# A graph-and-FFN kernel: the self-loop is added before the window's matmuls, GpSimd's order of work is turned round, and each edge gather gets its index copied first

## The reference

```
edge_index = stack([src, dst])                  # 206250 edges, sorted by dst
# graph layer on layernorm(x):
src, dst = edge_index + self-loops of all nodes
norm = dinv[src] * dinv[dst]                    # dinv = rsqrt(degree)
h    = layernorm(x) @ W
out  = segment_sum(h[src] * norm, dst) + b
x    = x + where(out > 0, out, prelu_a * out)
# FFN on layernorm(x): softmax router over 8 experts, the top 2 for all nodes,
# gelu(z @ W1[e] + b1[e]) @ W2[e] + b2[e], weighted sum, layer norm
x    = x + ffn(layernorm(x))
```

## Time and profile before

| | |
|---|---|
| median of 3 runs | 1114.66 us (1113.95 to 1115.24) |
| the profiled execution, its own time | 1114.66 us |
| its span in the profile | 1112.8 us |
| TensorE busy | 1082.8 us, 97% |
| VectorE busy | 935.0 us, 84% |
| GpSimd busy | 672.9 us, 60% |
| ScalarE busy | 537.8 us, 48% |
| the 40 windows | from about 84 us to 791 us |

### The profile page before, as it was taken

One profiled execution on the slowest core, in us unless ns is written; L12 is line 12 of the kernel. 1 busy time (PEld: TensorE's weight loads), 2 busy tenths in 40 slices (PEclk: granted clock), 3 DMA queues, 4 the chain that ended last, 5 costly groups with the idle time before them and its releaser, 6 DMA issues.

```text
span 1112.8 us, 21292 instructions
## 1 busy us (share of the span) xinstructions
PE 1082.8 (97%) x6833; PEld 930.4 (84%) x6834; DVE 935.0 (84%) x2198; ACT 537.8 (48%) x1367; POOL 672.9 (60%) x584
## 2 busy tenths in 40 slices
PE   6999999999999999999999999999899999999997
PEld 5787887888888888888888888888699999999997
DVE  6898888989989899898998998986468787878785
ACT  5794443444434444443444444444375564656451
POOL 3103677888888888888888888882124342434332
PEclk9999999999999999999999999999999999999999
DMA  8076454555455555555545555552211111111101
GB/s 281 17 293 217 117 145 134 154 148 162 137 150 147 152 157 145 162 145 155 154 138 159 145 154 146 153 146 76 81 59 58 44 42 46 48 39 52 38 24 33
DMA packets 65527, 134.96 MB, mean 121 GB/s; under 512 B 10388, under 2 KB 35870, under 8 KB 65438
## 3 DMA queue, kind: packets, MB, share of 16 engines
q0 software_dynamic: 29040, 93.22, 30.0%
q1 hardware_dynamic: 36398, 40.62, 11.2%
HBM read 108.14 MB, written 25.67 MB: 120 GB/s over the span
## 4 chain that ended last, share of the span: by engine, by line
PE 83%; DVE 6%; ACT 4%; issue 3%; DMA 1%; POOL 1%; DVEq 1%; ACTq 0%; POOLq 0%; SPq 0%
PE bank L1776 40%; PE bank L1753 14%; PE bank L1907 11%; PE bank L1794 8%; PE bank L1894 5%; PE bank L1644 2%; DVE gl L1344 2%; PE bank L1879 1%; ACT zf L1562 1%; ACT gf L1577 1%; POOL rstdf L797 1%; DMA W<-in_W 1%; ACT gh L1575 1%; PE bank L1741 1%; PE bank L1634 1%
## 5 line engine op out<-in xcount | busy, mean ns | idle before, releaser
L703 POOL DMA_INDIRECT row<-h_table,lists x315 | 435.3, 1382 | 101.1 <-issue 71.0
L1776 PE MATMUL bank<-tab,adj 128*128 128x512 f32 x1960 | 476.0, 392 | 1.1 <-ACT adj L1510 1.1
L1505 ACT CAST adj<-bank 128x392 fp32r<-128x392 f32 x624 | 258.0, 501 | 398.6 <-PE bank L1753 398.6
L1776 PEld LDWEIGHTS bank<-tab,adj 128*128 128x128 f32 x1960 | 366.4, 188 | 82.1 <-DVE tab L1021 1.2
L1126 DVE TENSOR_TENSOR hot_key<-iota_key,turned 128x588 bf16<-128x588 bf16 (+1 forms) x480 | 243.6, 559 | 0.0
L1118 DVE TENSOR_TENSOR hot_src<-iota_src,turned 128x1536 bf16<-128x1536 bf16 x160 | 157.6, 985 | 53.5 <-PE bank L1753 52.1
L1753 PEld LDWEIGHTS bank<-hot_key,hot_src 128*128 128x128 bf16 x1872 | 157.5, 145 | 40.9 <-issue 29.3
L1753 PE MATMUL bank<-hot_key,hot_src 128*128 128x147 bf16 x1872 | 185.5, 248 | 0.0
L1344 DVE TENSOR_TENSOR gl<-gf,gh 128x384 fp32r<-128x384 f32 (+1 forms) x136 | 116.8, 886 | 29.5 <-ACT gf L1577 29.1
L1575 ACT ACTIVATE gh<-bank,b1e 128x384 fp32r<-128x384 f32 (+1 forms) x136 | 78.3, 575 | 97.6 <-PE bank L1894 97.5
L1907 PE MATMUL bank<-W2h,gh 128*128 128x256 f32 x392 | 112.2, 286 | 0.0
(11 more groups left out here) (230 smaller groups left out, 1334.0 us busy)
## 6 DMA issues: line engine op xcount, KB each, us to landing
h_table<-tab SPq DMA_DIRECT2D x5, 2048.0 KB, 8.8
x1f<-x_dram POOLq DMA_DIRECT2D x16, 384.0 KB, 3.8
out<-res SPq DMA_DIRECT2D x48, 128.0 KB
xin<-in_x SPq DMA_DIRECT2D x45, 128.0 KB, 3.4
x_dram<-x SPq DMA_DIRECT2D x45, 128.0 KB
row<-h_table,lists POOLq DMA_INDIRECT x315, 3.8
xs<-in_x SPq DMA_DIRECT2D x2, 1536.0 KB, 15.1
h_table<-tab SPq DMA_DIRECT2D x1, 2304.0 KB, 14.3
```

What stands on the lines that cost most here:

```text
L703: g.indirect_dma_start(out=row[:, u, :].bitcast(F32), out_offset=None, in_=h_table, in_offset=bass.IndirectOffsetOnAxis(ap=lists[:, m % 2, ...
L1505: s.copy(adj[k][:, :].rearrange("p (q n) -> p q n", n=P)[:, :, at:at + GN], adj_ps[j][:, 0:KEYS].rearrange("p (n q) -> p q n", q=T)).then_ ...
L1776: last = mm(acc[k][:, :], adj[k][:, q * P:(q + 1) * P], tab[:, q, :], start=(at == 0), stop=(at == T - 1), skip_group_check=True)
```

## The change

Three things are changed. `load_edges(i)` first copies the column of 48 indices from `starts` into a small tile `edge_ix[k]` with a GpSimd copy, waits for that copy, and gives the tile to the indirect DMA. In `ends(i)`, `load_edges(i+4)` moves to the front, and the add of the self-loop moves to the end, behind the `add_z` and the gathers of steps 1 and 2 and ahead of the next window's `followers(i+1, 3)`; it is `add_loop(i+2)` there, so the adds keep their order, and `add_loop(1)` is issued before the loop. On TensorE the 49 matmuls of a window run in the plain order of blocks, and the wait for `loop_added` takes the place of the wait for `bank_kept` at s = 0 of the window.

```diff
+        edge_ix = [sb(f"edge_ix{k}", [ROWS, 1], I32) for k in range(2)]
+        edge_ix_ready = sem("edge_ix_ready")
...
                     pool.wait_ge(raw_free, i + 1)
+                    g.tensor_copy(edge_ix[k][:, :], starts[:, DENSE[i]:DENSE[i] + 1]).then_inc(edge_ix_ready, 1)
+                    pool.wait_ge(edge_ix_ready, i + 1)
                     g.indirect_dma_start(
...
-                        in_offset=bass.IndirectOffsetOnAxis(ap=starts[:, DENSE[i]:DENSE[i] + 1], axis=1),
+                        in_offset=bass.IndirectOffsetOnAxis(ap=edge_ix[k][:, :], axis=1),
...
                     d = DENSE[i]
+                    if i + 4 < ND:
+                        load_edges(i + 4)
                     for n in followers(i, STEPS - 1):
                         gather(n)
-                    if i + 1 < ND:
-                        add_loop(i + 1)
-                    if i + 4 < ND:
-                        load_edges(i + 4)
...
+                    if i + 2 < ND:
+                        add_loop(i + 2)
                     if d < BY_SP:
                         store_x1(d, d % 2)
...
                 add_loop(0)
+                add_loop(1)
...
-                def add_rows(i, lo, hi):
-                    k, d = i % 2, DENSE[i]
-                    order_of = [q for q in range(T) if q != d] + [d]
-                    for at in range(lo, hi):
-                        q = order_of[at]
-                        if q == d:
-                            pe.wait_ge(loop_added, i + 1)
-                        last = mm(acc[k][:, :], adj[k][:, q * P:(q + 1) * P], tab[:, q, :], start=(at == 0), stop=(at == T - 1), skip_group_check=True)
+                def add_rows(k, lo, hi):
+                    for q in range(lo, hi):
+                        last = mm(acc[k][:, :], adj[k][:, q * P:(q + 1) * P], tab[:, q, :], start=(q == 0), stop=(q == T - 1), skip_group_check=True)
...
                         if s == 0:
-                            pe.wait_ge(bank_kept, i * (STEPS * SG) + (STEPS * SG + SG))
+                            pe.wait_ge(loop_added, i + 1)
```

More of the change, by code:

```diff
@@ L1798, in window @@
                 def window(i):
+                    k = i % 2
                     for s in range(STEPS):
@@ L1809, in window @@
                         add_gathered(i, s)
-                        add_rows(i, cuts[s], cuts[s + 1])
+                        add_rows(k, cuts[s], cuts[s + 1])
                         if i == 0:
```

## The result

The changed kernel takes 1156.6 us, the median of 4 runs (1155.9 to 1161.6), against 1115.0 for the kernel before, the median of 4 (1114.0 to 1115.3). The ratio is 1.0384, with a 95% interval of 1.0354 to 1.0414. The change makes the kernel 3.8% slower. The direction was forecast, at 1137 with a range of 1118 to 1152; the measured time lies above the range, and the loss is almost twice the one forecast.

A forecast was written before the change was run, and what follows sets the result against it. The prediction took TensorE as always busy in the windows and GpSimd's queue as full. It added 7 us for the first windows and 15.5 for windows 7 to 37, 22.5 on 1114.66: 1137 us, range 1118 to 1152.

The forecast's parts named there:

- What bounds the kernel: TensorE busy 1082.8 of 1112.8 us, almost nothing to win back; GpSimd's queue full, some 13 us a pattern in stretched gathers.
- The first windows: TensorE's new waits for the add: 1 us in windows 0 and 1, 4.7 and 2.6 next, minus 1.3; together 7 us.
- The copy: Index copy and the wait on it in GpSimd's queue: 0.8 us a window, between 0.1 and 1.2.
- The worst case that the prediction set aside: By the skill's rule, a copy starting in a one-hot step could wait up to 0.95 + 1.30 us.
- What GpSimd can absorb: Stretched gathers take up part of the copies' 0.8 us; 0.5 us lost in each of windows 7 to 37, 15.5 us.
- one window of 15.9 us to be had again: GpSimd did the window from 287.18 to 303.07 in 2.0 us less than 17.9; such a gain once a pattern offsets copies.
- Rival 2: GpSimd's queue is full, nothing absorbed, more gathers caught: 25 to 37 us plus 7, 1147 to 1159 or above; chance 0.16.
- What is paid once: At the window's start, a late add costs TensorE once, since GpSimd works on; each time only GpSimd's need beyond 17.9 us.
- What costs nothing: The order of the 49 matmuls, and load_edges(i+4) at the front of ends(i), whose edges land earlier: no cost.
- The signs: Waits for the add near 20 us, in most windows up to 37 if sustained; GpSimd's add starting before TensorE's window or at its start.
- signs of being wrong: Copies much dearer, gathers caught far less in their new places, or the granted clock falling in TensorE's pauses.

The follow-up runs named there:

- small one-hot kernel: The changed kernel with VectorE's hot_src and hot_key comparisons cut from block 2 on to 8 source and 8 key columns; 1119.3 us, ratio 1.0014.

## Why the prediction was wrong, by its own steps

**What bounds the kernel: right.** TensorE had nothing to win back, GpSimd's queue was full in spite of a busy share of 60%, and the stretched gathers made it so. The small one-hot kernel shows the last of these.

**The first windows: right in the sum, in part by luck.** Forecast 7 us, measured 6.8 at window 6. The terms were others: in place of 4.7 us at window 5 and 2.6 at window 6 stood one wait of 4.0 us at window 4, where gathers of 3.17 and 1.52 us stood ahead of the add, 3.4 us at half clock behind it, and 0.5 us each for rows in window 5 and for the add of window 6.

```profile
157.89 1.08 PE L1794 MATMUL bank<-row,hot_row 128*128 128x512 f32 x3 [3.96 <-POOL adj L696]
```

**The copy: right in size.** Taken at 0.8 us a window, between 0.1 and 1.2. It was 0.44 for the copy (not 0.2) and 0.83 to its DMA (taken: 0.77, ahead of it 0.16 before), together 1.1. VectorE catches it at times, which raises its mean. The worst case that the prediction set aside, 0.95 + 1.30 us, does occur: this copy ended at 217.99, and the last `hot_key` of its step at 217.95.

```profile
215.72 2.27 POOL L684 COPY edge_ix<-starts 48x1 int32<-48x1 int32 x1
```

**What GpSimd can absorb: not where the loss came from.** The sum put all of the sustained loss down to the copies: of 0.8 us a window 0.3 to 0.8 come out at the end, and 31 x 0.5 = 15.5. From window 6 to the last of them it was 11.3 + 20.1 + 1.0 = 32.3 us, twice as much. The copies aren't the missing half. Alone, in the kernel before, they cost 20 us, 0.56 for each of 36 windows; taken out of the changed kernel they give back about 10 us, 0.3 a window. Both lie within 0.3 to 0.8. The reason given, one window of 15.9 us to be had again, isn't borne out: in the kernel before, that window stands beside one of 20.9 and evens it out, and of a copy that nobody waits for nothing is absorbed. Rival 2 (nothing absorbed, 1147 to 1159, 0.16) has the measured time in its range, but not for the reason that it names. It put 25 to 37 us down to the copies, which cost 10 to 20, and to more caught gathers, and the gathers got shorter, from 1382 to 1324 ns on average. That it hit is luck.

**What is paid once: this is the step that failed.** The text held that a late add is paid once, since GpSimd works on while TensorE stands, and for all but the copies the sum has 7 us. The changed kernel without the copies loses 2.9%, 33 us. The early wait alone, with no work added to any queue, costs 4.05%, 45 us. GpSimd doesn't work on: it stands for the casts and for buffers that TensorE frees, a term that the sum put at nothing. GpSimd's groups from the add for window 12 to the one for window 36, six patterns, first in the kernel before, then in the changed one:

```profile
L703 POOL DMA_INDIRECT row<-h_table,lists x210 | 295.7, 1408 | 59.6 <-issue 46.5 <-PE bank L1794 11.3 <-ACT zst L1494 1.8
L682 POOL DMA_INDIRECT raw<-in_pairs,starts x24 | 26.0, 1084 | 3.8 <-issue 3.6 <-PE bank L1794 0.2
L692 POOL TENSOR_TENSOR adj<-adj,ident 128x128 fp32r<-128x128 f32 x24 | 14.7, 612 | 0.5
...
L707 POOL DMA_INDIRECT row<-h_table,lists x210 | 280.6, 1336 | 72.1 <-issue 56.5 <-PE bank L1794 14.8 <-ACT zst L1499 0.9
L686 POOL DMA_INDIRECT raw<-in_pairs,edge_ix x24 | 24.6, 1025 | 19.7 <-POOL edge_ix L684 12.3 <-PE bank L1794 7.4
L696 POOL TENSOR_TENSOR adj<-adj,ident 128x128 fp32r<-128x128 f32 x24 | 13.4, 558 | 3.6 <-ACT adj L1510 2.1 <-issue 1.1
L684 POOL COPY edge_ix<-starts 48x1 int32<-48x1 int32 x24 | 7.7, 319 | 0.0
```

For a pattern that is: copies and their wait, (7.7 + 19.7 - 3.8) / 6 = 3.9 us more, where the prediction had 3.2; shorter gathers, (295.7 - 280.6) / 6 = 2.5 less, where it had 1.2 absorbed; and GpSimd's own standing ahead of gathers and adds, (72.1 - 59.6 + 3.6 - 0.5) / 6 = 2.6 more, where it had nothing. With 0.4 less at the edge loads and adds the balance is about 3.6; TensorE lost 20.1 / 6 = 3.35, and the forecast was 4 x 0.5 = 2.0. Without the standing, and all else the same, it would have come out below the forecast.

What the standing does can be told from the lateness. Before, GpSimd could be 4 to 9 us late and still come round within a pattern, long windows paid for by short ones. With the wait at the window's start the add can't begin before the casts and must be done some 3.6 us later. Short windows then end in waits of GpSimd, long ones in TensorE's, and what is lost in the one isn't found in the other. The early wait took away a cover of 9.9 us that was in use in every window; the prediction counted its loss once.

**What costs nothing: partly wrong.** The new place of `load_edges` was put at nothing because the edges land earlier. What stands behind it, the gathers of step 3, was not followed to who waits for them. The order alone costs 11 us, nearly all of it waits for rows.

**The parts together.** Copy 1.8%, order 1.0%, early wait 4.05% would be 6.9%; the whole is 3.8%. With the new order the early wait costs less than without it (2.9% against 4.05%); the likely reason is that the add then stands ahead of the gathers of step 3. Copy and order add up behind the late wait (1.8 + 1.0 against 2.65), and the early wait costs only 1.2% on top of them. So no part has a price of its own: each slows a queue that is full already, and whichever deadline comes first shows the loss, the rows' behind the late wait, the add's behind the early one.

**The signs.** The waits for the add were to be near 20 us, in most windows; they are 29.7 us, and from window 12 on in one window of four. The add was to end up ahead of TensorE's window, and does. Of its signs of being wrong one came true, the granted clock falls in or behind TensorE's waits; by the run with matmuls ahead of the wait that isn't where the time went. The gathers are caught less, though not far less, which goes against the loss.

**What stays open.** Which gathers are caught, and why it is one interval in four that has 6 to 7 us of stretching, was read in the timeline and not tried by moving a phase. The copy's falling price with the other parts in place (20 us alone, 10 us in the changed kernel) was not tested by itself, nor was the early wait with the copies and the old order. The part after the last window, whose code the change doesn't touch, is 4.6 us longer in the profile of after (326.7 against 322.1); in the other runs' profiles it varies between 322 and 329 us, so nothing is read into it.

## What to carry to other kernels

A queue whose idle time is only gaps between its own instructions is full, whatever its busy share says. What is added to it adds up from window to window, so every place behind an added instruction needs its own deadline looked up: here the add had 9.9 us to spare, and the gathered rows ran out first. Lateness that costs nothing isn't slack that is free; it may be what levels long and short stretches of a loop, and a wait moved to the front of each iteration takes it away in every iteration, not once. And before a fast stretch of a loop is counted as reserve, its slow stretches are to be added to it.

## What the runs showed of the hardware

VectorE's plain two-input comparisons (`tensor_tensor`, bf16, both inputs in SBUF) hold up GpSimd's indirect DMAs. Cutting only those took the mean of 315 gathers from 1324 to 1032 ns, and the longest from 3.4 to 1.4 us; the one-input comparisons beside them (`hot_row`) stayed as they were, 81.3 us of them:

```profile
L1153 DVE TENSOR_SCALAR hot_row<-iota,own_dst 128x128 fp32r<-128x128 f32 x315 | 81.3, 328 | 0.3
L1134 DVE TENSOR_TENSOR hot_key<-iota_key,turned 128x32 bf16<-128x32 bf16 (+2 forms) x480 | 64.6, 188 | 0.2
L1124 DVE TENSOR_TENSOR hot_src<-iota_src,turned 128x96 bf16<-128x96 bf16 (+1 forms) x160 | 40.2, 251 | 310.7 <-PE bank L1761 237.5 <-remote 72.4 <-issue 0.3
```

The page "SBUF — State Buffer" of the Trainium skill, section "Who interferes with whom", states that a VectorE instruction with two SBUF inputs contends with GpSimd instructions that read SBUF, and infers that descriptor generation isn't touched by it, since that needs the write side. The runs here don't agree with the inference: a gather caught beside `hot_src` takes up to 3.4 us instead of 1.01. But a gather here also reads its row numbers from SBUF (the tile `lists`), and no run tells whether that read or the making of descriptors is what is held up.

GpSimd's wait for its own last copy is not always dear: a second copy that waits for the first starts 0.05 us behind it, a DMA that waits for a copy 0.82 us behind it (the copies done twice, at 406 us).

In or just behind six of TensorE's waits of 2.5 to 4.0 us in the windows, though not at three others of 2.5 to 2.8 us, the granted clock fell to half, 1.2 of 2.4 GHz, for 3.4 us, with TensorE busy until the wait began. With some two microseconds of matmuls ahead of the wait, and 0.7 to 1.1 us of it left, it stayed up in six windows; in the seventh 2.2 us of wait were left, and it fell.
